# Two output banks, another opening and passage, and the steps for the next block one chunk later in the shared expert

## The chip, the cores and the metric

The kernel runs on one core of a Trainium2 chip. What counts is the time of one execution on the device in microseconds. The engines are TensorE (PE, with its weight loads as PEld), VectorE (DVE), ScalarE (ACT), GpSimd (POOL) and SyncE (SP, which here only issues DMAs).

## The reference, cut to what matters

4096 tokens of 256 numbers (64 sequences of 64) pass two layers, each of a cross attention over 64 context rows of 128 numbers per sequence and a mixture of experts:

```
x = x + tanh(g[0]) * attention_a(layernorm(x), ctx, fside)        # 32 heads of 8, rotary
x = x + tanh(f[0]) * ffn_a(layernorm(x))
x = x + tanh(g[1]) * attention_b(layernorm(x), ctx, mask)         # 16 heads of 128, 8 kv heads
x = x + tanh(f[1]) * ffn_b(layernorm(x))

# attention: softmax(q k^T * scale) v, then times Wo
# ffn_a:  logits = x Wr^T ; top 2 of 8 experts by softmax, weights normalised
#         out = sum over the two: (silu(x Wg^T) * (x Wu^T)) Wd^T, 176 wide
#             + sigmoid(x ws^T) * shared expert of the same form, 704 wide
# ffn_b:  top 2 of 8 by tanh(x Wg1^T) Wg2^T ; experts silu(x Wup^T + bup) Wdown^T + bdown, 128 wide
```

The output is x in float32. Where a product needs full precision the kernel splits both factors into a high part and a rest ("hi" and "lo") and adds three products.

## The kernel before, in words

x stays in SBUF as 32 tiles of 128 tokens. The work runs in six stretches: attention a (16 rounds of 2 tiles, to about 415 us in the profiled execution), the shared expert of the first mixture, called f0 (8 blocks of 4 tiles, to 677), its routed experts (71 tiles of sorted rows, to 836), a passage, attention b (16 rounds of 2 tiles, from 906 to 1524 us) and the second mixture, f1 (8 blocks). Each engine has its own written-out queue of instructions, and the queues meet only in counting semaphores; nothing is ordered by a planner. In both attentions `rounds` (L62) runs a first round, a loop over 14 and a last one.

**Attention a.** Each round handles 8 chunks n of heads, two to a pair p = n // 2. TensorE makes scores (L598), transposes the exponentials (L607), and in `outputs0` (L611) multiplies them by the values (L621) and by ones (L625); values and sums go to `bank[4]`. The first chunk of a pair may only write once the pair before is out of that bank (L618). ScalarE computes exponentials (L1187) and copies their transposes from PSUM (L1167). VectorE takes maxima (L1705) and subtracts them (L1711), does queries and keys with rotation (L1690, L1692), and in `weigh0` (L1714) inverts the sums (L1717) and multiplies (L1720). Statistics of x for the layer norm are made once for 8 tiles at a time by `moments_x` (L1670), with an inverse root of all of them (`rsqrt`, L1636); in the opening two pieces of them stand before `queries(0)` (L1780), two are in round 0 (L1750).

**f0.** A block has 6 chunks of gate-up (`gate_up_g`, L840) and of down (`down_g`, L852), each with a product and a low part on VectorE (L2079, L2085). The steps that prepare the next block are hung between the chunks at slots t named in `SLOTS` (L43): norm, turn 0 and 1 (`turn_g`, L672, matmul L680), logits, back and largest, weigh (counts and weights) and place (`place_g`, L827, matmul L832, with the slots that GpSimd scatters by, L1542). GpSimd splits the expert weights between scatters (L1550). `resid_g` (L2091) adds a finished block to x.

**Passage.** TensorE forms m = Wq Wk (L961) and n = Wo Wv products (L969), which wait for the DMAs of o1 and w1 (L964, issued at L499 and L500). VectorE takes their low parts (L2207, L2215). In between it adds the routed experts' rows, gathered by GpSimd (L1565), to tiles 0 and 1 (`add_tile`, L2165), with statistics and norm. Then ones are made (L2225), TensorE turns the first tiles (L989) and makes the queries (L536 to L538). Before the first round VectorE splits w1, the second mixture's weights, 4096 columns in one cast (L2323) and one subtraction (L2325).

**Attention b.** `attend1` on TensorE (L1059), ScalarE (L1401), GpSimd (L1572) and VectorE (L2262). VectorE takes maxima (L2266), subtracts (L2269), sums and scales; ScalarE copies high parts of probabilities (L1390) and outputs (L1397); GpSimd scales the probabilities (L1575) and gathers rows, and is idle most of a round.

## Time and profile before

| | us |
|---|---|
| median of 3 executions | 1811.49 |
| lowest, highest | 1809.84, 1813.02 |
| profiled execution | 1808.37 |
| its span, first to last instruction | 1806.6 |
| TensorE busy (matmuls) | 1620.6 (90%) |
| VectorE busy | 1167.7 (65%) |
| ScalarE busy | 735.4 (41%) |
| GpSimd busy | 411.5 (23%) |

The profile is of one execution. Its rows give start and length in us, the engine, the line of the kernel, the operation and its tiles; in square brackets stands how long the engine was idle before and what released it. A name such as "DVEq" is VectorE's sequencer. The mean granted clock of TensorE was 0.974 of full speed. Ends of matmuls are modelled and spans of GpSimd are rough.

### The profile page before, as it was taken

Reading aid. Unit: us, or ns where it says so; the run is one execution under the profiler, and the core shown is the slowest. Engines: PE = TensorE matmul, PEld = TensorE weight load, DVE = VectorE, ACT = ScalarE, POOL = GpSimd, SP = SyncE. Lnnn points to the kernel's source line nnn. Section 1 sums busy time; section 2 is a strip of 40 time slices with the busy share of each in tenths; the row PEclk is TensorE's granted clock in tenths of the full one; section 3 lists DMA queues with packets and bytes.
Section 4 is the critical chain, followed back from the end, with each engine's and each line's share of the span. In section 5 each row is a group of like instructions: output and inputs, shape, how many; then the busy total and the mean of one; then the engine's idle time right before and its main releaser. Section 6 shows DMA issues by size and latency. Waiting matters only on the chain.

```text
span 1806.6 us, 42368 instructions
## 1 busy us (share of the span) xinstructions
PE 1620.6 (90%) x14740; PEld 1362.5 (75%) x14740; DVE 1167.7 (65%) x3031; ACT 735.4 (41%) x1492; POOL 411.5 (23%) x448
## 2 busy tenths in 40 slices
PE   3899999978999899997799999999999997699998
PEld 2566666646777689997688888888888886588887
DVE  5877777785667655555666666666666654465655
ACT  2566666652232225554233333333333332344343
POOL 3555555531313310000112111122122101000000
PEclk9999999989999999999899999999999998799999
DMA  6666666651101014434000000000000000000000
GB/s 175 143 120 120 121 121 120 119 98 51 53 24 36 35 36 142 152 124 164 27 25 21 26 20 25 22 20 24 26 20 26 20 14 4 3 24 12 12 24 24
DMA packets 127356, 107.06 MB, mean 59 GB/s; under 512 B 10442, under 2 KB 120195, under 8 KB 127020
## 3 DMA queue, kind: packets, MB, share of 16 engines
q1 hardware_dynamic: 121068, 89.07, 20.9%
q0 software_dynamic: 6208, 16.95, 2.9%
q8 instruction: 47, 0.77, 0.2%
q14 instruction: 33, 0.27, 0.1%
HBM read 49.22 MB, written 56.77 MB: 59 GB/s over the span
## 4 chain that ended last, share of the span: by engine, by line
PE 54%; DVE 26%; issue 10%; ACT 6%; DMA 2%; DVEq 1%; ACTq 1%; SPq 0%; POOL 0%; POOLq 0%
PE bank L536 11%; PE bank L538 10%; PE bank L537 10%; PE bank L1015 4%; PE bank L607 2%; PE bank L621 2%; PE bank L598 2%; PE bank L1043 2%; DVE probs_b L2269 2%; DVE rm_b L2266 2%; PE bank L562 2%; PE bank L638 2%; DVE x L2170 1%; DVE oT_b_lo L2258 1%; PE bank L625 1%
## 5 line engine op out<-in xcount | busy, mean ns | idle before, releaser
L1575 POOL TENSOR_TENSOR probs_b<-probs_b,rs_b 128x512 f32<-128x512 f32 x64 | 66.8, 1043 | 483.1 <-DVE rs_b L2279 482.8
L1404 ACT ACTIVATE probs_b<-probs_b 128x512 f32<-128x512 f32 x64 | 40.4, 632 | 323.6 <-DVE probs_b L2269 323.6
L536 PE MATMUL bank<-xT_b_hi,m_hi 128*128 128x256 f32 x512 | 153.8, 300 | 20.0 <-ACT qT L1383 12.0
L536 PE MATMUL bank<-n_hi,oT_b_hi 128*128 128x256 f32 x512 | 150.0, 293 | 5.6 <-DVE x L2237 5.6
L537 PE MATMUL bank<-xT_b_hi,m_lo 128*128 128x256 f32 x512 | 145.8, 285 | 0.0
L538 PE MATMUL bank<-xT_b_lo,m_hi 128*128 128x256 f32 x512 | 145.6, 284 | 0.0
L537 PE MATMUL bank<-n_hi,oT_b_lo 128*128 128x256 f32 x512 | 145.3, 284 | 0.0
L538 PE MATMUL bank<-n_lo,oT_b_hi 128*128 128x256 f32 x512 | 145.3, 284 | 0.0
L1015 PEld LDWEIGHTS bank<-ctxT_b,qT 128*128 128x128 f32 x1024 | 126.5, 194 | 2.8
L1187 ACT ACTIVATE probs_a<-probs_a 128x512 f32<-128x512 f32 x128 | 80.3, 627 | 110.7 <-DVE probs_a L1711 110.2
L1015 PE MATMUL bank<-ctxT_b,qT 128*128 128x64 f32 x1024 | 123.0, 274 | 0.0
L2258 DVE TENSOR_TENSOR oT_b_lo<-bank,oT_b_hi 128x512 fp32r<-128x512 f32 x128 | 82.3, 684 | 61.7 <-ACT oT_b_hi L1397 61.7
L536 PEld LDWEIGHTS bank<-xT_b_hi,m_hi 128*128 128x128 f32 x512 | 98.7, 193 | 26.4 <-ACT qT L1383 15.0
L1565 POOL DMA_INDIRECT xn_b<-sorted_y,place_of x62 | 59.9, 966 | 236.8 <-DMA sorted_y<-ys 180.9
L2266 DVE TENSOR_REDUCE rm_b<-bank 128x8 f32<-128x512 f32 x64 | 44.2, 691 | 105.8 <-PE bank L1015 95.9
L536 PEld LDWEIGHTS bank<-n_hi,oT_b_hi 128*128 128x128 f32 x512 | 98.6, 193 | 13.4 <-DVE x L2237 6.7
L1383 ACT ACTIVATE qT<-bank 128x512 f32<-128x512 f32 x128 | 76.3, 596 | 67.5 <-PE bank L538 67.5
L1542 POOL DMA_INDIRECT sorted_x<-f_xn,f_slots x64 | 62.1, 970 | 182.6 <-DVEq L2030 165.2
L1705 DVE TENSOR_REDUCE rm_a<-bank 128x8 f32<-128x512 f32 x128 | 82.1, 683 | 32.4 <-PE bank L598 31.1
L537 PEld LDWEIGHTS bank<-xT_b_hi,m_lo 128*128 128x128 f32 x512 | 99.0, 193 | 0.0
L538 PEld LDWEIGHTS bank<-xT_b_lo,m_hi 128*128 128x128 f32 x512 | 98.9, 193 | 0.0
L537 PEld LDWEIGHTS bank<-n_hi,oT_b_lo 128*128 128x128 f32 x512 | 98.7, 193 | 0.0
(316 smaller groups left out, 4790.9 us busy)
## 6 DMA issues: line engine op xcount, KB each, us to landing
sorted_x<-zeros SPq DMA_DIRECT2D x16, 2112.0 KB, 14.6
xg<-sorted_x SPq DMA_DIRECT2D x71, 128.0 KB, 2.1
sorted_y<-ys SPq DMA_DIRECT2D x71, 128.0 KB, 1.9
w_raw<-in_w SPq DMA_DIRECT2D x16, 408.0 KB, 3.8
x<-in_x SPq DMA_DIRECT2D x4, 1024.0 KB, 7.3
cx_raw<-in_ctx SPq DMA_DIRECT2D x32, 128.0 KB, 2.7
out<-x SPq DMA_DIRECT2D x8, 512.0 KB, 2.9
ctxT_a<-in_ctxT SPq DMA_DIRECT2D x16, 128.0 KB, 2.1
```

The source lines that it names most:

```text
L536: pe.matmul(dst, lh, rh, start=start, stop=False, skip_group_check=True)
L537: pe.matmul(dst, ll, rh, start=False, stop=False, skip_group_check=True)
L538: return pe.matmul(dst, lh, rl, start=False, stop=stop, skip_group_check=True)
L1015: m = pe.matmul(bank[b % 2][:, g * S:(g + 1) * S], qT[:, b, 2 * g:2 * g + 2, :].rearrange("p h q -> p (h q)"), ctxT_b[:, b, :], start=Fals ...
L1187: act.activation(probs_a[t % NP], probs_a[t % NP], ACT.Exp, scale=SCALE0).then_inc(s["a_exp"], 1)
L1383: act.activation(qT[:, :, 2 * c:2 * c + 2, :].rearrange("p b h q -> p h b q"), bank[6 + c % 2][:, :].rearrange("p (h b q) -> p h b q", h=2 ...
L1542: pool.indirect_dma_start(out=xs_dram, out_offset=bass.IndirectOffsetOnAxis(ap=at, axis=0), in_=f0["xn"][i % 2][:, t, :], in_offset=None). ...
L1565: pool.indirect_dma_start(out=rows[:, c, :], out_offset=None, in_=ys_dram, in_offset=bass.IndirectOffsetOnAxis(ap=place_of[:, c, tile:tile ...
L1575: pool.tensor_tensor(probs_b[b], probs_b[b], rs_b[:, b, :].unsqueeze(2).broadcast_to([P, G1, S]), ALU.mult).then_inc(s["b_probs"], 1)
L1705: return st.done(ve.tensor_reduce(rm_a[:, n % 4, :], score_bank(n)[:, :].rearrange("p (h k) -> p h k", h=E), AX_X, ALU.max))
L2258: ve.tensor_tensor(oTl[:, b // 2, :, par, :, cols], bank[4 + par][:, :].rearrange("p (j u q) -> p j u q", j=4, u=2), oTh[:, b // 2, :, par ...
L2266: st.done(ve.tensor_reduce(rm_b[:, b % 2, :], sc, AX_X, ALU.max))
```

## The change: what it does

Five edits go together. (1) In f0, turn 0 and 1, logits, back and largest, and weigh stand one chunk later; norm and place stay. (2) Attention a's outputs of a pair go to bank 4 or 6 in turns; TensorE's wait is for one pair earlier, and VectorE's reciprocal waits for its own multiply of the pair before, as both use one buffer. (3) In the opening of attention a, the statistics of tiles 8 to 15 and their rsqrt move from before `queries(0)` to the first pair of round 0; each later piece moves by a pair. (4) In the passage the n products wait for o1 alone; w1's DMA is issued after the first round's context loads; VectorE takes n's first low part, adds tiles 0 and 1, takes two more low parts, does statistics and norm, and then the rest; TensorE's first turn doesn't wait for the ones or for n; `add_tile(3)` and `stats_b(1)` move behind the first `centre(0)`. (5) w1 is split in 16 pieces of 256 columns, one per round: a copy on ScalarE and a subtraction on GpSimd, in place of VectorE's two operations.

```diff
@@ -40,7 +40,7 @@
 NF = 8
 FT = NT // NF
 
-SLOTS = {"f0": dict(norm=0, t0=1, t1=2, logits=3, back=4, largest=4, weigh=5, place=7),
+SLOTS = {"f0": dict(norm=0, t0=2, t1=3, logits=4, back=5, largest=5, weigh=6, place=7),
          "f1": dict(norm=0, t0=1, t1=3, logits=4, back=5, largest=5, weigh=6, weights=8)}
 
 STEPS = {"a": 12, "b": 41, "f1": 58}
@@ -180,6 +180,7 @@
         m_hi, m_lo = w1.halves("m", H1, KT, P)
         n_hi, n_lo = w1.halves("n", H1, D)
         w1_hi, w1_lo, w1_raw = w1.split("w1", KT * HID1 + NC1 * D)
+        W1S = (KT * HID1 + NC1 * D) // NA
         valid = w1.take("valid", P)
         ctxT_b = w1.take("ctxT_b", 4, S)
         mrow_raw = w1.take("mrow_raw", 4 * S)
@@ -320,6 +321,9 @@
 
         def turned(i):
             return bank[6 if i else 7]
+
+        def out_bank(p):
+            return bank[4 + 2 * (p % 2)]
 
         def score_bank(n):
             return bank[n % 2]
@@ -497,12 +501,11 @@
                     load_weights(j - 4)
             sp.wait_ge(s["x_y_psum"], NJ)
             sp.dma_start(o1_raw.rearrange("p k n -> p (k n)"), a["wo1"]).then_inc(s["o1_loaded"], 16)
-            sp.dma_start(w1_raw, a["w1"]).then_inc(s["o1_loaded"], 16)
             sp.wait_ge(s["n_psum"], H1 // 2)
             sp.wait_ge(s["mask_ready"], 1)
             sp.dma_start(biases.rearrange("a (b k) -> (a b) k", b=B), maskrow[0:B, :]).then_inc(s["biases_stored"], 16)
             sp.wait_ge(s["biases_stored"], 16)
-            with sp.Fori(0, NA) as i:
+            def load_round1(i):
                 sp.wait_ge(s["b_scores"], START + i * 4)
                 sp.dma_start(ctxT_b.rearrange("p a b -> p (a b)"), a["ctxT"][:, ds(i * 256, 256)]).then_inc(s["b_ctx_loaded"], 16)
                 sp.dma_start(mrow_raw[0:1, :], biases[:, ds(i * 256, 256)]).then_inc(s["b_ctx_loaded"], 16)
@@ -510,6 +513,11 @@
                 for half in range(2):
                     sp.dma_start(cx_raw[64 * half:64 * half + 64, :, :],
                                  a["ctx"][ds(i * 4, 4), :, :].rearrange("b k c -> k b c")).then_inc(s["b_cx_loaded"], 16)
+
+            load_round1(0)
+            sp.dma_start(w1_raw, a["w1"]).then_inc(s["o1_loaded"], 16)
+            with sp.Fori(1, NA) as i:
+                load_round1(i)
             sp.wait_ge(s["b_resid"], START + NA * 2)
             sp.dma_start(f1["rw_raw"].rearrange("p k m -> p (k m)"), a["rw1"]).then_inc(s["sel1_loaded"], 16)
             sp.dma_start(f1["wg2"][0:E, :], a["wg2"]).then_inc(s["sel1_loaded"], 16)
@@ -615,14 +623,14 @@
                 if n % 4 == 0:
                     pe.wait_ge(s["a_v_ready"], START + i * 8 + 4 + n)
                 if hh == 0:
-                    pe.wait_ge(s["a_oT_ready"], START + i * 4 + p)
+                    pe.wait_ge(s["a_oT_ready"], START + i * 4 + p - 1)
                 for b in range(2):
                     for j in range(4):
-                        m = pe.matmul(bank[4][32 * j:32 * j + 32, 64 * b:64 * b + 64],
+                        m = pe.matmul(out_bank(p)[32 * j:32 * j + 32, 64 * b:64 * b + 64],
                                       v_bd[:, p // 2, hh, b, 4 * (p % 2) + j, :],
                                       pT_a[n % 2][:, j, 64 * b:64 * b + 64], start=(hh == 0 and b == 0), stop=(hh == 1), skip_group_check=True)
                 for j in range(4):
-                    m = pe.matmul(bank[4][32 * j:32 * j + 32, P:2 * P], total_a[:, hh, :], pT_a[n % 2][:, j, :],
+                    m = pe.matmul(out_bank(p)[32 * j:32 * j + 32, P:2 * P], total_a[:, hh, :], pT_a[n % 2][:, j, :],
                                   start=False, stop=(hh == 1), skip_group_check=True)
                 m.then_inc(s["a_o_psum"], 1)
 
@@ -961,7 +969,7 @@
                         m = pe.matmul(bank[c % 4][:, (2 * u + k) * P:(2 * u + k + 1) * P], q1_raw[:, 2 * c + u, k * P:(k + 1) * P],
                                       k1_raw[:, c, :], start=True, stop=True)
                 m.then_inc(s["m_psum"], 1)
-            pe.wait_ge(s["o1_loaded"], 32)
+            pe.wait_ge(s["o1_loaded"], 16)
             for c in range(H1 // 2):
                 if c >= 4:
                     pe.wait_ge(s["n_copied"], c - 3)
@@ -973,9 +981,6 @@
             pe.wait_ge(s["mask_ready"], 1)
             pe.wait_ge(s["m_copied"], H1 // 2)
             pe.matmul(bank[0][:, 0:B], valid[0:B, :], ident[0:B, 0:B], start=True, stop=True).then_inc(s["valid_psum"], 1)
-            pe.wait_ge(s["mask_ready"], 2)
-            pe.wait_ge(s["n_copied"], H1 // 2)
-            pe.wait_ge(s["mask_ready"], 3)
             NB = 4
 
             def turn_x1(i, first=False):
@@ -1093,8 +1098,10 @@
                 project1(i, 0, 0)
 
             turn_x1(0, first=True)
+            pe.wait_ge(s["n_copied"], H1 // 2)
             for c in range(H1 // 2):
                 queries1(0, c)
+            pe.wait_ge(s["mask_ready"], 3)
             rounds(pe, NA, attend1)
             outputs1(NA - 1, 3)
             project1(NA - 1, 0, 1)
@@ -1105,7 +1112,7 @@
             pe.wait_ge(s["sel1_cast"], 16)
             pe.wait_ge(s["sel1_loaded"], 48)
             pe.wait_ge(s["rw_split"], 2)
-            pe.wait_ge(s["w1_split"], 1)
+            pe.wait_ge(s["w1_split"], NA)
             hi, lo = ffn1_view(w1_hi), ffn1_view(w1_lo)
             ffn("f1", f1, NC1, HID1, None, (hi[0], lo[0]), (hi[1], lo[1]), None)
 
@@ -1426,6 +1433,8 @@
                 pth(i, 1)
                 next_q(3, 4)
                 oth(i, 1)
+                act.wait_ge(s["o1_loaded"], 32)
+                act.activation(w1_hi[:, ds(i * W1S, W1S)], w1_raw[:, ds(i * W1S, W1S)], ACT.Copy).then_inc(s["w0_hi"], 1)
                 pth(i, 2)
                 next_q(5, 6)
                 oth(i, 2)
@@ -1576,6 +1585,9 @@
                                        ALU.mult).then_inc(s["b_probs"], 1)
                     if i + 2 < NA and b % 2 == 1:
                         gather((i + 2) * 2 + b // 2)
+                pool.wait_ge(s["w0_hi"], START + NA + i + 1)
+                pool.tensor_tensor(w1_lo[:, i * W1S:i * W1S + W1S], w1_raw[:, i * W1S:i * W1S + W1S],
+                                   w1_hi[:, i * W1S:i * W1S + W1S], ALU.subtract).then_inc(s["w1_split"], 1)
             pool.wait_ge(s["b_resid"], START + NA * 2)
             pool.memset(f1["bd_raw"], 0.0).then_inc(s["bd_cleared"], 1)
             pool.memset(f1["sel"].bitcast(F32), 0.0).then_inc(s["sel_cleared"], 1)
@@ -1714,10 +1726,11 @@
             def weigh0(i, p):
 
                 ve.wait_ge(s["a_o_psum"], START + i * NS + 2 * p + 2)
-                st.done(ve.reciprocal(inv_a, bank[4][:, P:2 * P]))
+                ve.wait_ge(s["a_oT_ready"], START + i * 4 + p)
+                st.done(ve.reciprocal(inv_a, out_bank(p)[:, P:2 * P]))
                 ve.wait_ge(s["a_y_psum"], START + i * 2 + p // 2 - 1)
                 st.wait()
-                ve.tensor_tensor(oT_a[:, p, :], bank[4][:, 0:P], inv_a, ALU.mult).then_inc(s["a_oT_ready"], 1)
+                ve.tensor_tensor(oT_a[:, p, :], out_bank(p)[:, 0:P], inv_a, ALU.mult).then_inc(s["a_oT_ready"], 1)
 
             def resid0(i, u):
                 ve.wait_ge(s["a_bias"], START + i + 1)
@@ -1747,9 +1760,11 @@
                         centre0(i, 2 * p + hh, most[hh])
                     if p == 2 and not last:
                         queries(i + 1)
-                    if first and p < 2:
-                        moments_x(2 + p, 8 * p)
-                    if first and p == 1:
+                    if first and p < 3:
+                        moments_x(1 + p, 8 * (p // 2))
+                    if first and p == 0:
+                        rsqrt(rstd[:, 8:16], nmr[:, 8:16], 8, 8)
+                    if first and p == 3:
                         rsqrt(rstd[:, 16:32], nmr[:, 16:32], 8, 16)
                     if p >= 2:
                         weigh0(i, p - 2)
@@ -1779,8 +1794,6 @@
 
             ve.wait_ge(s["tables_loaded"], 64)
             keys(0)
-            moments_x(1, 0)
-            rsqrt(rstd[:, 8:16], nmr[:, 8:16], 8, 8)
             queries(0)
             attend0(0, first=True)
             ve.wait_ge(s["w0x_loaded"], 160)
@@ -2206,14 +2219,16 @@
                 ve.wait_ge(s["scalar_steps"], c + 1)
                 ve.tensor_tensor(m_lo[:, 2 * c:2 * c + 2].rearrange("p u k c -> p (u k c)"), bank[c % 4][:, :],
                                  m_hi[:, 2 * c:2 * c + 2].rearrange("p u k c -> p (u k c)"), ALU.subtract).then_inc(s["m_copied"], 1)
-            add_tile(0, more=1)
-            add_tile(1, yg1)
-            stats_b(0)
-            norm1(0)
             for c in range(H1 // 2):
                 ve.wait_ge(s["scalar_steps"], H1 // 2 + c + 1)
                 ve.tensor_tensor(n_lo[:, 2 * c:2 * c + 2, :].rearrange("p u n -> p (u n)"), bank[4 + c % 4][:, :],
                                  n_hi[:, 2 * c:2 * c + 2, :].rearrange("p u n -> p (u n)"), ALU.subtract).then_inc(s["n_copied"], 1)
+                if c == 0:
+                    add_tile(0, more=1)
+                    add_tile(1, yg1)
+                if c == 2:
+                    stats_b(0)
+                    norm1(0)
             ve.wait_ge(s["valid_psum"], 1)
             st.done(ve.tensor_copy(validb, bank[0][:, 0:B]))
             st.wait()
@@ -2280,7 +2295,10 @@
                                      ALU.mult).then_inc(s["b_recip"], 1)
 
                 centre(0)
-                if not first:
+                if first:
+                    add_tile(3)
+                    stats_b(1)
+                else:
                     otl(i - 1, 3)
                     resid1(i - 1, 0)
                 if not last:
@@ -2317,12 +2335,6 @@
             xT_low1(0)
             mask_row(0)
             add_tile(2)
-            add_tile(3)
-            stats_b(1)
-            ve.wait_ge(s["o1_loaded"], 32)
-            st.done(ve.tensor_copy(w1_hi, w1_raw))
-            st.wait()
-            ve.tensor_tensor(w1_lo, w1_raw, w1_hi, ALU.subtract).then_inc(s["w1_split"], 1)
             attend1(0, first=True)
             with ve.Fori(1, NA - 2) as i:
                 st.loop(i, STEPS["b"], 1)
```

## Rows read from the trace of the kernel before

**Rows 1.** The page, section 4: shares of the chain that ended last, by engine.

```profile
PE 54%; DVE 26%; issue 10%; ACT 6%; DMA 2%; DVEq 1%; ACTq 1%; SPq 0%; POOL 0%; POOLq 0%
```

**Rows 2.** Windows: start:end, length, busy us and instructions by engine, granted clock, DMA.

```profile
36.48:62.94 26.46, 18.63 (x266) 12.67 (x266) 25.36 (x76) 11.94 (x27) 13.59 (x17) 0.87 0.72 158
...
553.00:558.00 5.00, 4.88 (x16) 3.71 (x16) 4.85 (x3) 0.60 (x1) 4.80 (x2) 0.66 0.15 52
```

**Rows 3.** TensorE's waits, 60 to 400 us: in total, times, longest.

```profile
PE bank L621 <- DVE oT_a L1720: 15.8, 14, 1.1
```

**Rows 4.** Timeline of one round: start, length, engine, line, operation, out<-in, [idle<-releaser].

```profile
217.38 0.43 PE L621 MATMUL bank<-pT_a,v_bd 128*32 128x64 f32 x16 [1.13 <-DVE oT_a L1720]
...
220.11 0.58 ACT L1167 ACTIVATE pT_a<-bank 128x512 f32<-128x512 f32 x1
...
221.38 0.43 PE L621 MATMUL bank<-pT_a,v_bd 128*32 128x64 f32 x16
```

**Rows 5.** Timeline, opening of attention a, TensorE and VectorE.

```profile
22.84 3.68 PE L562 MATMUL bank<-xnT_a,wq 128*64 128x128 f32 x32 [0.69 <-ACT xnT_a L1144]
...
24.28 2.71 DVE L1674 BATCH_NORM_STATS2 bn<-x 128x6 f32<-128x256 f32 x8 [3.36 <-DMA x<-in_x]
...
31.09 0.01 DVE L1690 LOAD_MASK_SELECT qw_a<-bank  x1 [0.19 <-DVE nmr L1657]
...
36.48 1.29 DVE L1705 TENSOR_REDUCE rm_a<-bank 128x8 f32<-128x512 f32 x2 [4.07 <-PE bank L598]
...
53.35 1.09 PE L562 MATMUL bank<-xnT_a,wq 128*64 128x128 f32 x16
...
64.15 1.29 DVE L1705 TENSOR_REDUCE rm_a<-bank 128x8 f32<-128x512 f32 x2 [1.21 <-PE bank L598]
```

**Rows 6.** TensorE's waits, 400 to 645 us.

```profile
PE bank L680 <- DVEq L1736: 12.4, 7, 1.9
```

**Rows 7.** Timeline, blocks of the shared expert, TensorE and VectorE.

```profile
471.80 0.19 DVE L1979 COPY f_lg<-bank 128x36 f32<-128x36 f32 x1
...
475.31 0.68 DVE L2082 TENSOR_TENSOR f_s<-bank,f_s 64x512 f32<-64x512 f32 x1 [2.09 <-ACT f_s L1291]
...
476.52 0.16 DVE L1993 CAST f_ixf<-f_ix 128x8 f32<-128x8 uint32 x1
...
478.21 0.41 PE L832 MATMUL bank<-f_cnt,f_below 128*128 128x32 f32 x2 [0.71 <-DVEq L2007]
...
489.53 0.66 PE L680 MATMUL bank<-ident,f_xn 128*128 128x128 f32 x4 [1.88 <-DVEq L1736]
...
553.12 0.66 PE L680 MATMUL bank<-ident,f_xn 128*128 128x128 f32 x4 [1.89 <-DVEq L1736]
```

**Rows 8.** Timeline, fifth block of the shared expert, VectorE and GpSimd.

```profile
553.76 5.52 DVE L2088 TENSOR_TENSOR f_hl<-f_s,f_hh 128x512 fp32r<-128x512 f32 x1
...
554.16 4.56 POOL L1550 TENSOR_TENSOR w_lo<-w_raw,w_hi 88x2048 fp32r<-88x2048 f32 x1
```

**Rows 9.** TensorE's waits in the passage, 836 to 906 us.

```profile
PE bank L969 <- DMA w_raw<-in_w: 7.2, 1, 7.2
```

**Rows 10.** DMA issues, 830 to 906 us: KB each, us from issue to landing.

```profile
o_raw<-in_wo SPq DMA_DIRECT2D x1, 2048.0 KB, 8.5
```

**Rows 11.** Timeline of the passage, SyncE, VectorE and TensorE.

```profile
836.48 0.43 SPq L499 DMA_DIRECT2D o_raw<-in_wo  x1
...
851.34 1.00 DVE L2170 SCALAR_TENSOR_TENSOR x<-xn_b,wts,x 128x256 f32<-128x256 f32 x2 [6.36 <-DMA yg<-sorted_y,place_of]
...
858.64 3.23 DVE L2215 TENSOR_TENSOR n_lo<-bank,n_hi 128x512 fp32r<-128x512 f32 x5
...
865.76 0.63 PE L989 MATMUL bank<-ident,xn_b 128*128 128x128 f32 x4 [2.29 <-DVE ones L2225]
...
885.04 4.43 DVE L2325 TENSOR_TENSOR w_lo<-w_raw,w_hi 128x4096 fp32r<-128x4096 f32 x1
```

**Rows 12.** Timeline, a GpSimd operation on 128x256.

```profile
217.79 0.62 POOL L1467 TENSOR_TENSOR k_hd<-k_rot,headmask 128x256 f32<-128x256 f32 x1
```

## The prediction

> **What bounds the kernel now.** I read the shares of the chain that ended last first [rows 1]: TensorE has 54% of it and VectorE 26%, so a stall of TensorE that goes is time unless VectorE is next, and the next thing late has to be looked for each time. Then the windows by stage [rows 2] and TensorE's waits [rows 3, 6], which say what each stall waited for and how often (for the passage [rows 9]), and last the timelines around each edit [rows 4, 5, 7, 8, 11, 12]. The edits touch five places: the 16 rounds of attention a, its opening, the 8 blocks of the shared expert (f0), the passage into attention b, and the split of w1.
>
> **Two output banks (rounds 1 to 14 of attention a).** TensorE's L621 waits for VectorE's multiply L1720 once a round, 15.8 us in 14 [rows 3]; in the round read it is the first half of the second pair of head groups, 1.13 us until 217.38 [rows 4]. With the second bank this wait goes and that matmul starts near 216.2. What is late next is in the same view: TensorE would then reach the first half of the third pair 1.2 us early, at 220.2, but that needs ScalarE's copy L1167, 220.11 + 0.58 = 220.69 [rows 4], whose own start hangs on VectorE's maxima and not on this bank. So it starts at about 220.75 and not at 221.38: 0.63 us a round, not 1.13. 14 × 0.63 = 8.8, and some 0.5 in the last round: −9.3. Ends: 0, if the copy slips along with the round, and 14 × 1.13 = −15.8. I take the middle one because the copy is the nearest row. The wait that VectorE's reciprocal gets is for its own multiply of the pair before, met over 2 us ago each time; behind it stand reductions whose results TensorE waits for, but it costs nothing.
>
> **Opening of attention a.** 8 tiles' statistics and their rsqrt go from before queries(0) into round 0. Before: queries(0) were out of TensorE at 22.84 + 3.68 = 26.5, VectorE took them at 31.09, and the first maxima came at 36.48 after 4.07 idle [rows 5]. Without the moved work, the first maxima come 4.4 us earlier, at 32.1. But from 36.48 to 62.94 VectorE was never free (25.36 of 26.46 us busy, the rest is issue [rows 2]), so what is moved in there is paid in full: the pair took 31.09 − 24.28 − 0.15 = 6.66 us [rows 5]. And the step of queries(1) now comes before the statistics of tiles 24 to 31 and the long rsqrt, while TensorE's second half of queries(1) started at 53.35 for 1.09 us [rows 5], and its predecessors only move up by 1.2: VectorE would be there at 50.8 and takes it at 53.4, 2.6 us idle. So 32.1 + 26.46 + 6.66 + 2.6 = 67.8, and round 1 begins at about 68.0 in place of 64.15, whose own idle 1.21 [rows 5] is swallowed: +3.85. Ends: −4.4, if all of it were hidden behind waits, and +6.8 if the queries idle 5.5. TensorE, granted 0.87 in that stretch [rows 2], waits for VectorE in both orders.
>
> **Shared expert (f0), seven passages between blocks.** The turn of the next block's tiles waited 12.4 us in 7 [rows 6], 1.88 in the one read [rows 7], for the normalised tiles; one chunk later these are long done, and the wait goes. The chunk that now stands there (gate-up 2) needs the product of chunk 0; VectorE reaches this earlier by the 0.6 of one low part that moved ahead of the count, so about 0.1 of wait is left. What takes its place is at the end of the block: largest (471.80 to 473.2, 1.42 us) stood in the shadow of gate-up 5, and now stands behind it. Gate-up 5 ended at 474.65; the product follows at 475.31 [rows 7], then from 475.92 a low part 0.60, largest 1.45, the other low part 0.60, and the count 478.21 − 476.52 = 1.69 [rows 7]: the place matmul comes 5.75 us after gate-up 5, not 3.56. TensorE has two down chunks (2.85) and the back turns (0.34) to do in it, so it idles there for some 2.6 us instead of 0.71 [rows 7], which the trace shows eight times at 0.3 to 0.8. New period: 5.75 + 9.44 (place to gate-up 2, as before, 478.21 to 489.53 − 1.88) + 16.56 (gate-up 2 to the end of gate-up 5, less the back turns) = 31.75, against 31.8 (two blocks from 489.53 to 553.12 [rows 7]). So 0 per passage, between −1.88 (the place step doesn't move) and +2.2 (the turn's wait comes back): −13 to +15.4 in 7. I take 0.
>
> **The two collisions in f0.** In blocks 4 and 5 VectorE's L2088 takes 5.52 us beside GpSimd's L1550 of 4.56 [rows 8], where it takes 0.68 otherwise, and each of these blocks is longer by about as much; the granted clock falls to 0.66 in 553 to 558 [rows 2]. Both instructions hang on the place step and both move by about the same 0.5 us towards the block's start, so I leave them colliding: 0, with ±1.7 each for what the order of the step next to them gives or takes.
> The Trainium skill says in "SBUF — State Buffer", section "Who interferes with whom", that a VectorE instruction with two SBUF inputs and a GpSimd one that reads SBUF exclude each other for their whole length; the two rows agree. By that rule the 16 new subtractions on GpSimd speak against this change; what they would do is the fifth rival below.
>
> **Passage into attention b.** Before: o1's and w1's loads were issued together, the n products waited for both (7.2 us for w1 [rows 9]), and the gathers of tiles 0 and 1, issued beside them, landed 6.5 us after issue, so that VectorE added only at 851.34 [rows 11]. New, from these rows: o1 lands at 836.48 + 8.5 = 845 [rows 10, 11], n products start there; the gathers land near 848.4 without w1 beside them; VectorE's n_lo(0) to 848.6, two adds to 850.4, n_lo(1) and (2) to 851.6, statistics and norm (5.1: from 851.34 to 858.64 less the two adds' 2.1 and an issue) to 856.75, n_lo(3) at once, TensorE's last n product to 859, n_lo(7) 860.9, ones 861.4, and the low half of the first turned tile at 862.1. The turn itself (865.76, after 2.29 for ones [rows 11]) no longer waits for them. Queries(0) start 5.7 us earlier. Then the split of w1, whose subtraction alone is 4.43 [rows 11] and whose cast before it 2.3, leaves VectorE's path ahead of the first maxima, and add(3) with its statistics, 5.5 us, moves behind centre(0) and takes their place: the second scores wait for it nearly as long as before. That gives 0.5 more: −6.2. On SP's queue w1's load now stands behind the first round's context loads, which therefore don't wait for it, and its first user is ScalarE's piece in round 0, over 20 us later. It runs beside the gathers of tiles 2 and 3; if they take 6.5 us again, VectorE still has some 6 us before it needs them. Ends −4 (the gathers are not quicker) and −8.
>
> **w1's split in 16 pieces.** Per round of attention b a 256-column copy on ScalarE, under 0.6 (the 512-column copy took 0.58 [rows 4]), ahead of the copy of probabilities for which TensorE is not late (it has over 1.5 us), and a subtraction of 0.61 on GpSimd (an operation on 128x256 takes that [rows 12]), which idles most of each round. 0 for 15 rounds, +0.2 in the last, at worst 16 × 0.4 = +6.4.
>
> **Sum.** −9.3 + 3.85 + 0 + 0 − 6.2 + 0.2 = −11.5 us. The profiled execution took 1808.37 (span 1806.6), so 1796.9 for such a one. It lies 3.1 us below the median of the three runs, 1811.49; I forecast for a median: 1800.0. What a measurement of this kernel can tell from no change is about 0.2%, 3.6 us.
>
> **Rivals.**
> 1. *Slower: VectorE's queue becomes the bound of f0.* The place step grows as worked out, and the product of chunk 0 comes so late that gate-up 2 waits as long as the turn did. For it: that product stands right behind the resid step, and the old turn's wait ended on VectorE. Against: the old wait was for the norm, 1.4 us behind the product. The sum passes +3.6 from a wait of gate-up 2 of 1.7 us: −11.5 + 7 × 1.7 + 3.2. Price 7 × 1.88 + 2 × 1.6 in the collision blocks = 16.4: 1796.9 + 16.4 + 3.1 = 1816.4.
> 2. *The copy slips, the banks give nothing.* +9.3: 1809.3. For it: a round of VectorE is 75% busy; against: the exponentials and copies hang on maxima that start when TensorE's scores are there, and these come earlier.
> 3. *The place step stays hidden* (the count gets through by the time the downs end), f0 keeps −13: 1787. Against: largest, 1.42 us, has nowhere else to stand.
> 4. *The opening hides the moved work*, −4.4 for +3.85: 1791.8. For it: TensorE works on queries(1) earlier than I have it; against: VectorE was full.
> 5. *GpSimd's pieces block VectorE in attention b*, 0.61 × 15 = +9: 1809. In the round read, the VectorE steps near the piece take one input from PSUM, so they shouldn't collide.
> 6. The change moves the time by less than 3.6 for reasons spread over all this: 1811.
>
> **Chances.** Forecast 0.50 (its own range 1795 to 1804), rival 1 0.08, 2 0.10, 3 0.10, 4 0.12, 5 0.05, 6 0.05. The second rival lies 2.2 us below the median of before, so it is half "same": faster 0.77, same 0.15, slower 0.08. Range: 1788 to 1809, which leaves out rival 1, rival 6 and most of 3.
>
> **What would show it.** L621's wait for L1720 gone in rounds 1 to 14 and its wait for the copy near 0.5 to 1.1; round period 22.0 for 22.6. Round 1's first maxima at 68 for 64.15. In f0 the turn's wait gone, L832's wait near 2.6, block period 31.8, longer by 5.3 twice. First queries of attention b 5.7 us earlier relative to the last expert tile. Attention b's period 40.2 unchanged. If f0's period moves by over 0.5, or the round's by under 0.3, the forecast is wrong in that term.

## The result, and the profile after

The changed kernel takes 1807.26 us (median of 20, 1801.48 to 1811.43) against 1810.89 (median of 20, 1809.37 to 1813.02) for the one before: ratio 0.9975, 95% interval 0.9966 to 0.9984. It is 3.6 to 4.5 us faster where 11.5 were forecast. The forecast of 1800.0 lies below all 20 runs (the fastest took 1801.48), though the range held the median. The spread has grown from 3.7 to 10 us. The profiled execution has a span of 1805.9 against 1806.6.

The stages, each read from the first instruction of the next one in the timelines of the two profiled executions:

| stage | before, us | after, us | difference | forecast |
|---|---|---|---|---|
| to the first maxima of round 1 | 64.15 | 66.46 | +2.31 | +3.85 |
| attention a, rounds 1 to 15 | 352.67 | 341.35 | −11.32 | −9.3 |
| f0, first gate-up to first expert tile | 260.26 | 274.11 | +13.85 | 0 |
| expert tiles | 159.15 | 159.13 | 0 | 0 |
| passage, to the fourth maxima of attention b | 67.59 | 60.78 | −6.81 | −6.2 |
| attention b from there | 642.59 | 643.53 | +0.94 | +0.2 |
| f1 | 260.19 | 260.54 | +0.35 | 0 |

They add up to −0.7, the difference of the spans. One row is far off, f0's. In the page of the changed kernel (busy us and share by engine, and the chain by engine) TensorE is busy 11 us longer with the same 14740 matmuls [rows 1 has the chain before]:

```profile
PE 1631.7 (90%) x14740; PEld 1371.8 (76%) x14740; DVE 1161.5 (64%) x3029; ACT 738.3 (41%) x1508; POOL 423.4 (23%) x464
...
PE 56%; DVE 22%; issue 10%; ACT 6%; SPq 2%; DVEq 1%; DMA 1%; ACTq 1%
```

Instructions that are the same and take longer point at TensorE's clock. I went there by the waits, first those of the shared expert, 400 to 645 us (total, times, longest):

```profile
PE bank L840 <- DVEq L2020: 14.4, 7, 2.4
...
PE bank L688 <- DVEq L1749: 4.0, 2, 2.5
...
PE bank L544 <- DVE f_s L2095: 0.8, 3, 0.4
```

The turn's wait, 12.4 in 7 [rows 6], is gone but for the two blocks with a collision; gate-up 2 waits 0.8 in all; and the place matmul waits 2.34 in each block for 0.71 [rows 7]. All that was forecast. Then the block between two turns (453 to 487; start, length, engine, line, operation):

```profile
452.91 0.60 PE L688 MATMUL bank<-ident,f_xn 128*128 128x128 f32 x4
...
472.21 0.41 PE L840 MATMUL bank<-f_cnt,f_below 128*128 128x32 f32 x2 [2.34 <-DVEq L2020]
...
473.47 0.28 PE L544 MATMUL bank<-w_hi,f_hh 128*128 128x256 f32 x1
...
474.17 0.42 PE L545 MATMUL bank<-w_hi,f_hl 128*128 128x256 f32 x1
...
479.46 0.63 PE L545 MATMUL bank<-f_xT_hi,w_lo 128*128 128x512 f32 x1
...
481.10 0.39 PE L544 MATMUL bank<-f_xT_hi,w_hi 128*128 128x512 f32 x1
...
487.25 0.60 PE L688 MATMUL bank<-ident,f_xn 128*128 128x128 f32 x4
```

The period is 487.25 − 452.91 = 34.34 us where 31.75 was forecast. Behind the place matmul the same kind of 128x256 matmul that took 0.28 takes 0.42, and one of 512 columns 0.63 where it takes 0.39 at the end. The windows behind six of the seven place matmuls show why (start:end, length, busy us by engine; the third number from the right is the granted clock):

```profile
440.00:446.00 6.00, 6.00 (x21) 5.00 (x20) 5.38 (x27) 0.00 (x0) 4.65 (x5) 0.50 0.30 109
...
472.40:479.40 7.00, 7.00 (x32) 6.23 (x32) 6.13 (x33) 0.00 (x0) 3.99 (x5) 0.59 0.17 59
...
541.00:548.00 7.00, 7.00 (x32) 6.26 (x33) 6.13 (x33) 0.00 (x0) 3.98 (x5) 0.57 0.16 56
...
580.00:587.00 7.00, 7.00 (x30) 6.46 (x30) 5.81 (x31) 0.00 (x0) 3.86 (x4) 0.50 0.17 59
...
617.90:625.00 7.10, 7.10 (x44) 6.20 (x44) 6.04 (x32) 0.60 (x1) 4.16 (x5) 1.00 0.16 58
...
650.00:657.00 7.00, 7.00 (x31) 6.17 (x31) 2.76 (x11) 0.00 (x0) 4.24 (x5) 0.58 0.19 67
```

Behind six of the seven (the one not shown, at 506.54, too) TensorE went to 0.50, which is 1.2 GHz, for most of the window; behind one (617.9) it stayed at 1.00, 2.4 GHz, though the wait ahead of it was 2.35 as well. In the kernel before no place matmul shows that:

```profile
478.60:485.00 6.40, 6.40 (x41) 5.58 (x41) 5.67 (x29) 0.03 (x1) 3.36 (x4) 1.00 0.18 60
...
510.40:517.00 6.60, 6.60 (x41) 5.76 (x41) 5.84 (x30) 0.23 (x1) 3.56 (x4) 1.00 0.16 60
```

A clock of 0.58 over 7 us with TensorE always busy leaves 0.42 × 7 = 2.9 us of work undone at full speed, of which the block shows 2.6. These falls (stretches at 0.50) don't all cost the same. From place matmul to place matmul, the three undisturbed blocks behind a fall are longer than before by 2.65, 2.53 and 2.49 us (34.3 for 31.8), the two with a collision by 1.82 and 0.88, and from the last place matmul to the first expert tile it is 3.03: 13.4 of the 13.85 us by which f0 grew. The one block whose clock stayed up, with the same waits at both of its ends, takes 649.56 − 617.64 = 31.92 us, close to the 31.75 forecast:

```profile
617.64 0.41 PE L840 MATMUL bank<-f_cnt,f_below 128*128 128x32 f32 x2 [2.35 <-DVEq L2020]
...
649.56 0.41 PE L840 MATMUL bank<-f_cnt,f_below 128*128 128x32 f32 x2 [2.34 <-DVEq L2020]
```

The Trainium skill describes such a pattern on its page "TensorE: Matmul & The Clock Gate", in "HAM oscillation — how this bites in real kernels", for a kernel that waits for DMA between its bursts of matmuls: the clock falls in each wait, and the transition is paid for each time and not once. Six of these seven blocks agree with that in kind, and the one at 617.9 does not. The waits of the page are for DMA and longer than 2.34 us, so that a wait this short has the same effect is what these traces show.

The other stages, in rows that answer to those of before. Opening [rows 5], VectorE's timeline: first maxima, queries(1) and round 1.

```profile
31.25 1.29 DVE L1717 TENSOR_REDUCE rm_a<-bank 128x8 f32<-128x512 f32 x2 [4.07 <-PE bank L606]
...
52.71 0.01 DVE L1702 LOAD_MASK_SELECT qw_a<-bank  x1 [2.72 <-PE bank L570]
...
66.46 1.29 DVE L1717 TENSOR_REDUCE rm_a<-bank 128x8 f32<-128x512 f32 x2 [0.45 <-DVE f_rw_lo L1802]
```

Attention a [rows 3], TensorE's wait for the copy: in the table of waits from 60 to 400 us nothing is left of L621's wait for VectorE, 15.8 us before. The wait for ScalarE's copy was 9.1 in 14 before.

```profile
PE bank L629 <- ACT pT_a L1174: 17.2, 29, 0.7
```

The collision in f0 [rows 8], VectorE and GpSimd:

```profile
551.90 6.46 DVE L1646 TENSOR_SCALAR f_xn<-x,rstd,nmr 128x256 f32<-128x256 f32 x4
...
552.64 4.59 POOL L1559 TENSOR_TENSOR w_lo<-w_raw,w_hi 88x2048 fp32r<-88x2048 f32 x1
```

The passage [rows 11], TensorE and VectorE: n products, first queries, first maxima, and the add that moved behind them.

```profile
849.59 4.58 PE L977 MATMUL bank<-o_raw,v_raw 128*128 128x256 f32 x20 [1.16 <-DMA o_raw<-in_wo]
...
866.37 0.55 PE L544 MATMUL bank<-xT_b_hi,m_hi 128*128 128x256 f32 x1 [1.62 <-DVE xT_b_lo L2246]
...
882.62 0.69 DVE L2281 TENSOR_REDUCE rm_b<-bank 128x8 f32<-128x512 f32 x1 [7.22 <-PE bank L1020]
...
884.03 1.00 DVE L2183 SCALAR_TENSOR_TENSOR x<-xn_b,wts,x 128x256 f32<-128x256 f32 x2
```

The 16 pieces on GpSimd (line, count, busy us, mean ns):

```profile
L1589 POOL TENSOR_TENSOR w_lo<-w_raw,w_hi 128x256 fp32r<-128x256 f32 x16 | 11.9, 741 | 20.1 <-ACT w_hi L1437 20.1
```

### The profile page after: what moved, and what is told of

The parts are those of the page before. It is cut to its first block, busy times and chain, and to the rows that moved or that the text cites. A ratio compares the mean times of both kernels' runs of the same rounds, so it can differ in the third digit from the quotient of the medians.

```text
span 1805.9 us, 42480 instructions
## 1 busy us (share of the span) xinstructions
PE 1631.7 (90%) x14740; PEld 1371.8 (76%) x14740; DVE 1161.5 (64%) x3029; ACT 738.3 (41%) x1508; POOL 423.4 (23%) x464
## 4 chain that ended last, share of the span: by engine, by line
PE 56%; DVE 22%; issue 10%; ACT 6%; SPq 2%; DVEq 1%; DMA 1%; ACTq 1%
PE bank L544 12%; PE bank L545 10%; PE bank L546 10%; PE bank L1020 3%; PE bank L606 3%; PE bank L615 2%; PE bank L1048 2%; PE bank L629 2%; PE bank L570 2%; DVE rm_b L2281 2%; PE bank L646 2%; DVE rs_b L2289 2%; DVE probs_b L2284 1%; DVE oT_b_lo L2273 1%; DVE x L2183 1%
## 5 line engine op out<-in xcount | busy, mean ns | idle before, releaser
L1298 ACT ACTIVATE f_s<-bank 128x512 f32<-128x512 f32 (+1 forms) x48 | 28.7, 597 | 178.5 <-PE bank L546 178.5
```

## The experiments

Chips differ: on some the kernel before takes 1811 us, on others 1825 (its median beside each group of runs is given). Where two ratios are compared across chips, that is said. "Ratio" is to the kernel before on the same chip, with its 95% interval.

| run | edit | chip, before there | median, us | ratio |
|---|---|---|---|---|
| c_before | the kernel before | 12, 1811.1 | 1810.8 | 0.9997 (0.9987 to 1.0007) |
| c_after | the changed kernel | 12, 1811.1 | 1809.5 | 0.9983 (0.9970 to 0.9995) |
| e6_half_filled | 9 matmuls ahead of the wait | 12, 1811.1 | 1792.7 | 0.9898 (0.9882 to 0.9913) |
| e5_combined | order changed, see below | 12, 1811.1 | 1788.5 | 0.9871 (0.9855 to 0.9887) |
| e1_slots_back | old slots | 6, 1824.8 | 1810.6 | 0.9923 (0.9908 to 0.9937) |
| e2_slots_alone | new slots alone | 6, 1824.8 | 1832.1 | 1.0040 (1.0025 to 1.0054) |
| e3_filled | 18 matmuls ahead of the wait | 6, 1824.8 | 1799.5 | 0.9863 (0.9846 to 0.9880) |
| e4_place_behind_down | place behind down 4 | 6, 1824.8 | 1800.2 | 0.9868 (0.9850 to 0.9885) |
| e7_banks_alone | two banks alone | 2, 1825.8 | 1817.4 | 0.9945 (0.9930 to 0.9960) |
| e8_passage_alone | passage and w1 pieces alone | 2, 1825.8 | 1820.2 | 0.9962 (0.9948 to 0.9975) |
| e9_combined_filled | e5 and 7 matmuls | 2, 1825.8 | 1795.5 | 0.9830 (0.9815 to 0.9844) |
| e10_slots_back_again | old slots | 2, 1825.8 | 1815.2 | 0.9935 (0.9922 to 0.9949) |
| e11_combined_again | e5 | 9, 1825.8 | 1794.0 | 0.9819 (0.9798 to 0.9840) |
| e12_combined_filled_again | e9 | 9, 1825.8 | 1795.2 | 0.9832 (0.9809 to 0.9854) |
| e13_slots_alone_again | new slots alone | 9, 1825.8 | 1836.3 | 1.0057 (1.0034 to 1.0079) |
| e14_slots_back_third | old slots | 9, 1825.8 | 1811.2 | 0.9919 (0.9895 to 0.9943) |

**Is it the idle time or the order? The wait filled with work.** The fills leave the order and every wait on VectorE as they are; TensorE only has something to do.

```diff
                         if t == at["place"]:
+                            pe.wait_ge(s["g_slots_ready"], i + 1)
+                            for _ in range(18):        # e6_half_filled: 9
+                                pe.matmul(bank[4][:, D:2 * D], hi[2][0:P, SHARED, 0:P], hi[2][0:P, SHARED, :],
+                                          start=True, stop=True, skip_group_check=True)
                             place_g(i + 1)
```

> The changed kernel with 18 extra matmuls (128x128 weights, 256 columns, results not used) ahead of the place matmul's wait for the counts, so that TensorE is busy in most of the 2.34 us; nothing waits less. Clock theory: granted clock stays 1.00 behind the place matmul, blocks take about 31.8 instead of 34.3 us, f0 about 14 us less, median near 1794. Rival (the order itself costs the time: VectorE's chain is longer, and the idle time is only its mark): no change or a little slower, 1807 to 1809.

> The changed kernel with 9 extra matmuls ahead of the place wait instead of 18, so TensorE idles about 1.2 us there. If an idle stretch as short as those of the kernel before (0.7 to 1.9 us) doesn't lower the clock, it is as fast as with 18, near 1799. If what counts is that TensorE is less busy around that point, the clock falls in some blocks: 1803 to 1805.

> The changed kernel beside the others on one chip. Clock theory: slower than the filled one by 8 to 15 us, near 1808 to 1812, with a granted clock of 0.5 to 0.6 behind at least five of the seven place matmuls. Rival (the chip makes them alike): 1800.

With 9 extra matmuls in each of seven waits, so with more work and not less, the kernel is 16.8 us faster than the changed one on the same chip (1792.7 against 1809.5). The place matmul now waits 1.3, and two of them are 31.72 us apart, where 31.75 was forecast for the change itself (timeline, TensorE):

```profile
437.04 0.41 PE L840 MATMUL bank<-f_cnt,f_below 128*128 128x32 f32 x2 [1.30 <-DVEq L2023]
...
468.76 0.41 PE L840 MATMUL bank<-f_cnt,f_below 128*128 128x32 f32 x2 [1.26 <-DVEq L2023]
```

The windows behind the place matmuls:

```profile
469.00:476.00 7.00, 7.00 (x43) 6.10 (x43) 6.13 (x33) 0.48 (x1) 4.04 (x5) 1.00 0.17 59
...
501.00:508.00 7.00, 7.00 (x42) 6.06 (x42) 6.13 (x32) 0.60 (x1) 4.36 (x5) 1.00 0.20 71
...
606.00:613.00 7.00, 7.00 (x41) 6.04 (x41) 5.89 (x31) 0.60 (x1) 4.49 (x5) 1.00 0.22 77
```

The clock is 1.00 behind all seven. So the order costs nothing and the long idle stretch costs all of f0's loss; the rival, that VectorE's longer chain takes the time, is out. f0 is 259.6 us here, 260.3 before. With 18 matmuls the clock also stays behind all seven (0.2 us of wait), but two blocks of that run take 33.83 us and not 31.75: TensorE waits 1.9 and 2.0 in them for VectorE's product, which waits for ScalarE. e6 has no such wait on chip 12; that it comes with the chip (below) is argued, not shown. A third block takes 35.80, and TensorE stands still 3.5 us in it with nothing in the profile to release it.

**The same from the other side: the work that is there anyway.** One chunk of down goes ahead of the place matmul.

```diff
-                        if t == at["place"]:
-                            place_g(i + 1)
                     elif t == 1:
                         total_g()
                     if t >= 3:
                         down_g(i, t - 3)
+                    if i + 1 < NF and t == at["place"]:
+                        place_g(i + 1)
```

> The changed kernel with the place matmul behind down chunk 4 instead of ahead of it: the counts come as late as now, but TensorE has 1.42 us more to do before it waits. Clock theory: wait 0.9 us, the clock stays 1.00, some wait comes behind gate-up 1 since VectorE's chain from the counts to the next product is as long; blocks 31.8, median near 1794. Rival (the order costs the time): the time of the changed kernel, 1807.

TensorE's wait in f0 (total, times, longest) and two windows behind place matmuls:

```profile
PE bank L840 <- DVEq L2020: 6.6, 8, 0.9
```

```profile
474.50:481.00 6.50, 6.50 (x35) 5.52 (x35) 5.70 (x30) 0.60 (x1) 3.83 (x4) 1.00 0.18 63
...
507.00:513.50 6.50, 6.50 (x34) 5.53 (x34) 5.67 (x30) 0.60 (x1) 3.88 (x5) 1.00 0.17 61
```

The wait is 0.9, and the clock stays behind six of the seven (behind the one at 575.09 it is 0.74 over 6.5 us). It takes 1800.2 us beside 1799.5 for the filled kernel. Both are 6 us above the 1794 expected, on a chip of the slower kind; that they agree with each other is what tells.

**The slots alone, and the slots taken back.** One line, `SLOTS["f0"]`, set to the new values in the kernel before, or back to the old ones in the changed kernel.

> The kernel before with the new slots alone. Clock theory: f0 goes from 260 to 272 to 276 us, median near 1823, spread of some 10 us, place wait 2.3 us in each block, granted clock about 0.55 in the 6.5 us behind it. Rival (the loss needs the rest of the change): within 3 us of the kernel before.

> The kernel before with the new slots alone. On a chip where the kernel before takes 1811 us: f0 goes from 260 to 274 us by the clock falling behind six of seven place matmuls, 1822 to 1825, ratio 1.006 to 1.008. On a chip where it takes 1825: ratio 1.004 as measured. Rival: without the other edits the clock doesn't fall, ratio 1.000.

> The changed kernel with the shared expert's old slots (turn 1 and 2, logits 3, back and largest 4, weigh 5), the rest of the change kept. Clock theory (the 2.34 us for which TensorE now waits ahead of the place matmul drops its granted clock from 1.00 to 0.50 for the next 7 us in six of seven blocks, which is where f0's +13.85 us come from): f0 takes 260 us again, about 14 us less than the changed kernel, median near 1794, and the spread of the runs shrinks from 10 us to the 3.5 us of the kernel before. Rival (f0's loss came from what the earlier stages changed, such as scatters or memory traffic shifted against f0): f0 stays near 270 us, median above 1803.

> The changed kernel with the shared expert's old slots, once more, on another chip than the first time, where engines stood still for 10 us in one block with no semaphore outstanding. Clock theory: f0 near 260 us, 13 to 16 less than the changed kernel: 1794 to 1796, ratio 0.991 to the kernel before. Rival (the old slots don't go with the rest of the change: the standstill comes back, or the clock falls behind the turn's wait of 1.9 us): 1805 to 1811 as on the first chip.

> The changed kernel with the old slots. On a chip where the kernel before takes 1811 us: f0 near 260 us, 1794 to 1797, ratio 0.991 to 0.992. On one where it takes 1825: ratio 0.992 to 0.9935 as measured. Rival (the old slots don't go with the rest of the change): ratio 0.997 as for the change.

Alone the new slots cost 7 and 10 us (1.0040, 1.0057), less than the 14 that the first two traces show, but with the same sign and in the same place: the clock falls behind seven of seven place matmuls in e2 and six of seven in e13, with 2.3 us of wait ahead of each. The windows behind three place matmuls of e2:

```profile
487.40:494.00 6.60, 6.60 (x28) 6.14 (x29) 5.44 (x29) 0.00 (x0) 3.75 (x4) 0.50 0.18 63
...
523.20:530.00 6.80, 6.80 (x31) 5.97 (x31) 5.93 (x32) 0.00 (x0) 4.02 (x5) 0.59 0.16 58
...
557.60:564.00 6.40, 6.40 (x30) 5.66 (x30) 5.60 (x30) 0.00 (x0) 3.83 (x4) 0.58 0.17 61
```

Taken back they leave 0.9923, 0.9935 and 0.9919, against 0.9975 and 0.9983 for the changed kernel on other chips: 7 to 12 us. In these three traces no place matmul is followed by a fall (0.7 us of wait, 21 of 21). I had expected medians near 1794; all three runs landed on chips where the kernel before takes 1825, and no run shows the old slots with the other edits on the kind of chip where it takes 1811.

**What is different on those chips.** This wasn't part of the question, but the numbers can't be read without it.

> The kernel before once more, for its trace on this chip, where it took 1824.8 us beside the four kernels above and not 1810.9. Theory S (on this chip some engines' instructions arrive late in the shared expert, a stall of 3 to 12 us, and the clock then falls behind it): f0 takes 270 to 280 us in place of 260, with idle stretches that no semaphore ends, the other stages as in the first trace. Rival (this chip is slower throughout, or in the clock of all stages): all stages longer in proportion, 0.7%.

Chip 12 turned out to be of the first kind, so the kernel before was never profiled on the other kind, and its 14 us there aren't located by a trace of its own. Five kernels with the old slots were. In e1, TensorE, VectorE and ScalarE in the second block:

```profile
457.70 1.11 PE L688 MATMUL bank<-ident,f_xn 128*128 128x128 f32 x4 [11.72 <-DVEq L1749]
...
453.46 1.66 DVE L2107 SCALAR_TENSOR_TENSOR x<-bank,f_sg,x 128x256 f32<-128x256 f32 x4 [9.62 <-remote]
...
454.90 1.08 ACT L1298 ACTIVATE f_s<-bank 128x512 f32<-128x512 f32 x2 [20.08 <-remote]
```

TensorE waits 11.72 us for the turn, VectorE stood idle 9.62 and ScalarE 20.08, released by nothing that the profile sees ("remote"), while GpSimd's scatters went on. The traces of e7, e8, e10 and e14 have the same 11.9 to 12.0 us at the same place; with e1's these are three chips. Those with the new slots have idle times of that kind there too, 3 to 8 us on VectorE where there is one. It isn't that block alone: from 400 to 700 us ScalarE's activations L1298 (L1291, L1294 or L1301 in the others) stood idle 17 to 88 us in total with "remote" or "issue" as the releaser in each of the twelve traces from chips 6, 2 and 9, and not at all in the two first traces and the four of chip 12. That the engines' own instructions come late there would fit; it is argued, not shown. It hits the old slots harder, which would explain why the slots alone cost 7 to 10 there and not 14.

**The other two parts alone.**

```diff
# e7: the kernel before with
+        def out_bank(p):
+            return bank[4 + 2 * (p % 2)]
-                    pe.wait_ge(s["a_oT_ready"], START + i * 4 + p)
+                    pe.wait_ge(s["a_oT_ready"], START + i * 4 + p - 1)
...
# e8: the changed kernel with bank[4], the old opening and the old slots
```

> The kernel before with the two output banks alone. From the two traces the rounds of attention a are worth 0.62 us each and the last one 2.6 more: 11.3 us less, ratio 0.9938. As the prediction had it: 9.3 less, 0.9949. Rival (the banks are only worth it together with the new slots or opening, since what follows the stage catches it): under 4 us.

> The passage and the w1 pieces alone, with the old bank, the old opening and the old slots. From the traces 6.8 us less in the passage and 0.9 more in attention b: 5.9 less, ratio 0.9967. The prediction had 6.0. Rival (the pieces on GpSimd and ScalarE take it back): within 2 us of the kernel before.

0.9945 is 10.0 us (7.3 to 12.8), 0.9962 is 6.9 us (4.6 to 9.5). Both lie on the forecast terms of 9.3 and 6.0, and both rivals are out. The opening was not run alone; its +2.3 is read from the table of stages. 10.0 + 6.9 less 2.3 is 14.6, and c_before against e6, where f0 is neutral, gives 18 on its chip; the 3.5 between them are within the intervals.

**A version that beats both.** The changed kernel, with place behind down 4 as above, the old opening, and VectorE's statistics of the block after next moved from behind the slots to slot 3:

```diff
+                        if t == 3 and i + 2 < NF:
+                            stats_g(i + 2)
                         if t == at["place"]:
                             slots_g(i + 1)
-                            if i + 2 < NF:
-                                stats_g(i + 2)
```

> The changed kernel with the place matmul behind down chunk 4, the statistics of the block after next moved from behind the slots to slot 3 (VectorE's 5.0 us), and the old opening of attention a. Opening: 2.3 us less than the changed one. f0: the place wait 0.9 us, no wait behind gate-up 1, since VectorE goes from the slots to resid and the product: period 30.3 for 31.8. By the clock theory 1799.5 less 2.3 less 10 is 1787. Rival (VectorE's chain moves its wait elsewhere, or a later step catches it): 1797.

1788.5, ratio 0.9871: 23 us under the kernel before on the same chip and 21 under the changed one. The undisturbed block is 29.8 us long (467.82 to 497.62), a little under the 30.3 expected. But the clock fell behind five of the seven place matmuls (the expectations below say four), with only 0.9 us of wait ahead of them. Three of the windows:

```profile
468.20:475.00 6.80, 6.80 (x37) 5.76 (x37) 4.03 (x14) 0.60 (x1) 3.98 (x5) 1.00 0.17 60
...
498.00:505.00 7.00, 7.00 (x31) 5.79 (x31) 2.82 (x11) 0.58 (x1) 4.19 (x5) 0.76 0.18 64
...
529.00:536.00 7.00, 7.00 (x26) 5.85 (x27) 3.16 (x12) 0.00 (x0) 3.85 (x5) 0.60 0.16 56
```

> The combined kernel (place behind down chunk 4, early statistics, old opening), with 7 extra matmuls in the 0.9 us that TensorE waits ahead of the place matmul. In the combined kernel the clock fell in four of seven blocks all the same. If that 0.9 us of idle is what lowers it, the clock stays 1.00 and the blocks take 29.8 us each: 5 to 6 us less than 1788.5, near 1783. If the clock falls there for another reason (TensorE now works nearly without a pause), nothing changes or it falls in more blocks: 1788 to 1791.

> The combined kernel once more, beside the filled one: ratio 0.987 to the kernel before on a chip where that takes 1811, as measured. The clock falls behind the place matmul in three to five of seven blocks, whose length is then 31.3 and not 29.8 us.

> The combined kernel with 7 extra matmuls in the 0.9 us wait. If the wait is what lowers the clock: no fall behind the place matmul, 4 to 6 us less than the combined kernel beside it. If not: the same time within 2 us.

On chip 9 the two are equal, 1794.0 and 1795.2, so filling 0.9 us gained nothing there. It did take the falls away: the clock stays behind all seven place matmuls in e12 and in e9, while in e11 it fell behind two (576.98 and 611.34, 0.74 over 6.5 us each). The profiled execution of e11 is its slowest of four, 1800.7, so the others may have had fewer. In its blocks of 31.0 us the unfilled kernel kept its clock (windows of e11):

```profile
480.00:486.50 6.50, 6.50 (x35) 5.50 (x35) 3.76 (x14) 0.60 (x1) 3.85 (x4) 1.00 0.18 63
...
511.00:517.50 6.50, 6.50 (x34) 5.52 (x34) 3.74 (x13) 0.60 (x1) 3.84 (x4) 1.00 0.17 62
```

In those blocks the second turn waits 1.0 us for ScalarE and VectorE, which it doesn't in the 29.8 us blocks of chip 12. My expectation for e12 was half wrong: the falls went, the time stayed. Why 0.9 us is followed by a fall five times in e5, twice in e11 and once in e4 stays open, and what a fall costs in these kernels does too, since no filled twin was run on chip 12.

## Why the prediction was wrong, point by point

- **Two banks: right.** 0.62 us a round were measured from the round starts (21.96 for 22.58), 0.63 forecast, and TensorE's wait moved to ScalarE's copy as the chain said, 17.2 us in 29 (9.1 in 14 before). The rest of the 11.3 is at the two ends: round 1 gave 1.5 (64.15 to 87.67 before, 66.46 to 88.44 after) and the last one 1.7 instead of 0.5, not looked into. e7 puts the whole at 10.0.
- **Opening: right in kind, priced a little too dear.** Maxima at 31.25 (32.1 forecast), the idle 2.72 ahead of queries(1) (2.6 forecast), round 1 at 66.46 (68.0). The edit costs, as forecast, because VectorE had no free time there.
- **Passage: right.** Queries(0) 6.3 earlier (5.7), the whole 6.8 (6.2), e8 6.9. o1 landed 8.3 after issue, and n products waited 1.16.
- **w1's pieces: right.** They took 0.74 each on GpSimd, not 0.61, and attention b is 0.94 longer in all (0.2 forecast); the fifth rival, +9, didn't happen.
- **The collisions: as large as before, with another partner.** It is now the norm, 6.46 for four operations that take 1.37, that GpSimd's 4.59 blocks. I had left the low part in that role. "SBUF — State Buffer" in the Trainium skill, "Who interferes with whom", counts tensor_scalar among the operations that can take the shared ports; these rows agree.
- **f0: here it failed.** The step is the sum of the new period, "5.75 + 9.44 (place to gate-up 2, as before ...) + 16.56 ... = 31.75". Its structure was right: the waits came out at 2.34 (2.6 forecast), 0 and 0.1, and e6 has 31.72. What was mis-sized is the 9.44: from the place matmul to gate-up 2 it was taken from a trace in which TensorE ran at 2.4 GHz. I merged two idle pieces, 0.71 and 1.88, into one of 2.34, called the sum equal, and priced it at its length. In that stretch it cost another 2.5 to 2.65 us in an undisturbed block, and 13.4 in all behind six falls of seven. Without it the sum holds (e6, 31.72, and the block at 617.64, 31.92). I had the granted clock in front of me for two places (0.66 beside the collision, 0.87 in the opening [rows 2]) and took it there for a feature of the place and not for what a stall does. None of the six rivals had it; the first, a slower f0, had the sign and the size of f0's loss and the wrong mechanism. The trace of the kernel before holds more of it than the prediction read: two of its six turn waits of 1.8 to 1.9 us are followed by a fall, both in the blocks of the collisions. These are three windows of 4 us from such a turn on, in all of which TensorE is busy throughout; the first shows no fall:

```profile
521.34:525.34 4.00, 4.00 (x22) 3.41 (x23) 1.98 (x3) 1.15 (x3) 0.96 (x1) 1.00 0.19 68
553.12:557.12 4.00, 4.00 (x14) 3.19 (x14) 3.96 (x2) 0.60 (x1) 3.92 (x2) 0.61 0.18 66
590.21:594.21 4.00, 4.00 (x14) 3.22 (x15) 3.97 (x2) 0.60 (x1) 3.92 (x2) 0.67 0.18 66
```

- **Spread.** The changed kernel's runs spread over 10 us (12 on chip 12), those before over 3.7 (7.7 on chip 12), those of e3 to e6 over 2 to 3.5, but they are only four each, and e2 and e13, which have the falls, spread over 6 and 2.9. A fall more or less is about 1 to 3 us. That the number of falls makes the spread is argued, not shown: both traces of the changed kernel have six.

## What to carry to other kernels

An idle stretch of TensorE has two prices: its length, and what the work behind it costs at the lower clock. When a reorder trades two short stalls for one long one of the same sum, read the granted clock behind each stall of either kind, and put the longer price into the sum; here 2.34 us of wait cost 2.6 more. Where a wait can't be shortened, put work of the same engine into it first (a chunk that is due anyway, as in e4), before shortening any chain; where only 0.9 us of wait was left, filling it gained nothing (e12). And a step that is moved behind the last work that hid it should be moved together with something that can take that work's place.

## What the runs showed of the hardware that I had not expected

- Useless matmuls made the kernel faster: 9 in each of seven waits, −16.8 us on one chip.
- A wait of 2.3 us ahead of the place matmul was followed by a lower clock 25 times in 28: six of seven in both traces of the changed kernel (the same one spared in both, 617.6, and 618.2 in c_after), seven in e2, six in e13. A wait of 0.7 was never (49 place matmuls of seven traces), 1.26 never in e6; 0.9 was five times in e5, twice in e11 and once in e4, of seven each. The turn's 1.9 was twice of six in the first trace and three times of six in c_before (524.53, 593.38 and 630.47), whose profiled execution, 1817.2, was its slowest. The length of the wait isn't the whole rule.
- The kernel before takes 1811 us on some chips and 1825 on others, and in the kernels profiled on the latter up to three engines stand still in f0, most in its second block and there for 3 to 20 us, with nothing in the profile to release them. A change is to be compared with the kernel before on the same chip, or its sign can come from the chip.
